# Four graph layers on one core: features kept times 2048, statistics behind the last additions, and pass one's first four tiles summed by portions

## The reference

```
x += segment_sum(w[e] * gate(h) * (h @ W0) [src], dst)                          # layer 0
x += segment_sum(h[src], dst) @ W1.T + b1                                       # layer 1
agg = segment_sum(concat(h[src], h[dst]) @ Wm + bm, dst)
x += concat(h, agg) @ Wu + bu                                                   # layer 2
e = B_inv * segment_sum((h @ W3)[src], dst);  y = D_inv * segment_sum(e[dst], src) + b3
x += relu(batchnorm(y))                                                         # layer 3
```

## Time and profile before

| | us |
|---|---|
| median of 3 runs | 2575.72 (2571.42 to 2576.82) |
| the profiled execution | 2590.25 |
| its span, first to last instruction | 2588.4 |
| TensorE busy | 2311.7 (89%) |
| VectorE busy | 1599.1 (62%) |
| ScalarE busy | 1218.6 (47%) |
| mean granted TensorE clock | 0.958 of full |

### The profile page before, as it was taken

How to read it: one execution, slowest core, us unless ns; L and a number is a source line. 1 busy time by engine, 2 the same in 40 slices (tenths; PEclk the granted TensorE clock), 3 DMA queues, 4 the chain that set the end, 5 groups by cost and what they waited for, 6 DMA issues and landing times. The chain is left out here.

```text
span 2588.4 us, 71075 instructions
## 1 busy us (share of the span) xinstructions
PE 2311.7 (89%) x27901; PEld 1993.6 (77%) x27901; DVE 1599.1 (62%) x3654; ACT 1218.6 (47%) x2644; POOL 45.6 (2%) x51
## 2 busy tenths in 40 slices
PE   2489899999989998999938999899998999999997
PEld 2368788878778887887837888788887888887786
DVE  6689999999999998999962333234433222122223
ACT  2478787877778886887732222222232000011112
POOL 3300000000000000000000000000000000000000
PEclk9589999999999999999979999999999999999998
DMA  6579999999999999999999999899997999999997
GB/s 190 110 152 204 208 208 207 215 217 210 201 193 216 213 213 201 196 215 209 207 229 232 283 284 281 227 260 259 260 258 203 290 288 290 274 246 245 256 267 186
DMA packets 1608975, 589.27 MB, mean 228 GB/s; under 512 B 964422, under 2 KB 1605450, under 8 KB 1608567
## 3 DMA queue, kind: packets, MB, share of 16 engines
q1 hardware_dynamic: 1604869, 579.88, 100.7%
q0 software_dynamic: 1600, 4.92, 0.7%
q10 hardware_dynamic: 2226, 0.62, 0.2%
HBM read 255.26 MB, written 89.20 MB: 133 GB/s over the span
## 5 line engine op out<-in xcount | busy, mean ns | idle before, releaser
L1182 ACT CAST stage<-ps 128x784 f16<-128x784 f32 x784 | 656.5, 837 | 108.5 <-DMA counts_by_source<-stage 69.5
L655 PE MATMUL ps<-Ha,a_tiles 128*128 128x258 f16 x4802 | 548.2, 274 | 46.4 <-ACT Ha L1229 38.9
L655 PEld LDWEIGHTS ps<-Ha,a_tiles 128*128 128x128 f16 x4802 | 469.9, 98 | 116.5 <-ACT Ha L1229 39.1
L608 PE MATMUL ps<-hot_c,hot_r 128*128 128x98 f16 x3136 | 509.8, 212 | 13.6 <-DVE hot_c L890 7.3
L609 PE MATMUL ps<-hot_c,hot_r 128*128 128x98 f16 x3136 | 504.1, 211 | 0.0
L610 PE MATMUL ps<-hot_c,hot_r 128*128 128x98 f16 x3136 | 502.3, 210 | 0.0
L1167 ACT CAST stage<-ps 128x392 f16<-128x392 f32 x784 | 398.8, 509 | 141.5 <-PE ps L591 141.5
L583 PE MATMUL ps<-g_in,wt 128*128 128x128 f16 x2401 | 431.4, 222 | 34.7 <-DVE X L902 18.2
L584 PE MATMUL ps<-g_in,wt 128*128 128x128 f16 x2401 | 429.4, 222 | 0.0
L585 PE MATMUL ps<-g_in,wt 128*128 128x128 f16 x2401 | 429.2, 222 | 0.0
L902 DVE SCALAR_TENSOR_TENSOR X<-ps,X 128x512 f32<-128x512 f32 (+1 forms) x637 | 391.6, 649 | 52.1 <-PE ps L585 51.9
(11 more groups left out here) (195 smaller groups left out, 2039.8 us busy)
## 6 DMA issues: line engine op xcount, KB each, us to landing
a_tiles<-counts_by_source SPq DMA_DIRECT2D x147, 1600.0 KB, 8.8
counts_by_source<-stage SPq DMA_DIRECT2D x49, 1600.0 KB, 8.0
gated_parts<-G SPq DMA_DIRECT2D x7, 448.0 KB, 3.6
g_in<-gated_parts SPq DMA_DIRECT2D x98, 32.0 KB, 3.1
out_x<-X SPq DMA_DIRECT2D x12, 256.0 KB
edge_table<-tab SPq DMA_DIRECT2D x1, 2448.0 KB, 10.5
wt<-stage SPq DMA_TRANSPOSE x98, 10.9
dst_run<-in_dst SPq DMA_DIRECT2D x1, 612.4 KB
```

The lines of the kernel that those rows point to most:

```text
L608: mm(into(0), rows_, codes(0), start=v == 0, stop=True, skip_group_check=True)
L655: last = mm(ps[:, c % 2, 0:PARTS], a_slot(ph, c, i), moving[:, i], start=i == 0, stop=i == TILES - 1)
L1182: a.copy(stage[:, b, 0:2, 0:TILES, u * SET_COLS:(u + 1) * SET_COLS], of).then_inc(s("hi_done"), 1)
```

## The change

- Features are kept times 2048. The standard deviation is taken of var / 2048^2 + eps / 2048^2, so `rstd`, `nmr` and all features come out times 2048. The high part is the value times 1/2048 in float16, and one VectorE instruction (scalar_tensor_tensor, high * -2048 + value) writes the low part straight to Ha or Hb. ScalarE's low parts (L1208, L1229, L1258), the buffer `dbig` and the waits between them go. To make up for it `w_h` is multiplied by 1/2048, in one instruction ahead of the build, and `binv` by 2048.
- Statistics stand between the additions of tile 48: those of group g - 1 behind the addition of group g.
- Pass one: sums of the first four tiles are made together, each in a bank of its own. TensorE waits for the loads of all four, then for one portion at a time, and does the seven matmuls of that portion for each of the four tiles. Their transposes and weights follow after that.

The places left out repeat the same with `sum_bank`, drop the allocation of `dbig` and rename semaphores.

```diff
@@ -40,6 +40,7 @@
 LOW = 2048.0
+TOGETHER = 4
 WIDE = P + 2
@@ -93,6 +94,11 @@
     return (ph - 1) * TILES + c
+
+
+def sum_bank(ph, j, c):
+
+    return j if ph == 1 and isinstance(j, int) and j < TOGETHER else c % 2
...
@@ -470,6 +475,7 @@
             g.memset(cols[:, 5:6], EPS).then_inc(s("eps"), 1)
+            g.memset(cols[:, 6:7], EPS / (LOW * LOW)).then_inc(s("eps"), 1)
             g.memset(pad_rows[0:1, 0, :], 0).then_inc(s("pads"), 1)
@@ -640,9 +646,24 @@
+                    def first_tiles():
+
+                        for j in range(TOGETHER):
+                            pe.wait_ge(s(f"a_in{load_at(1, j) % SLOTS}"), (load_at(1, j) // SLOTS + 1) * 16)
+                        for part in range(SET):
+                            pe.wait_ge(s("h_ready1"), part + 1)
+                            for j in range(TOGETHER):
+                                for i in range(part * SET, (part + 1) * SET):
+                                    last = mm(ps[:, sum_bank(1, j, j), 0:PARTS], a_slot(1, j, i), Ha[:, i], start=i == 0, stop=i == TILES - 1, skip_group_check=True)
+                                if part == SET - 1:
+                                    last.then_inc(s("sum_done1"), 1)
+
                     def step(j, k, c, ph=ph, moving=moving):
                         q = c % SLOTS
-                        if on(j) and not general:
+                        if ph == 1 and not general and isinstance(j, int) and j < TOGETHER:
+                            if j == 0:
+                                first_tiles()
+                        elif on(j) and not general:
                             if ph == 4:
...
@@ -682,7 +703,8 @@
                     else:
-                        pe.wait_ge(s(f"h_ready{ph}"), SET if ph == 1 else TILES)
+                        if ph > 1:
+                            pe.wait_ge(s(f"h_ready{ph}"), TILES)
                     if not (general and ph == 3):
...
@@ -911,6 +933,12 @@
+                def row_stats(g):
+
+                    dve.wait_ge(s("added"), FOURS * (TILES - 1) + g + 1)
+                    for i in range(4 * g, min(4 * g + 4, TILES)):
+                        v.bn_stats(stats[:, i], X[:, i])
+
                 if general:
@@ -919,8 +947,11 @@
                     dve.wait_ge(s("g_x"), 1)
+                    for j in range(TILES):
+                        v.bn_stats(stats[:, j], X[:, j])
                 else:
                     dve.wait_ge(s("g_parts"), SET)
+                    v.tensor_scalar(w_h[:], w_h[:], 1.0 / LOW, None, ALU.mult)
                     tiles_loop(dve, build, 0)
@@ -928,22 +959,18 @@
                             add_four(t, t % 2, g)
-                    dve.wait_ge(s("added"), FOURS * TILES)
-                for j in range(TILES):
-                    v.bn_stats(stats[:, j], X[:, j])
-
-                def split(ph):
-
-                    if ph == 1:
-                        counts_stored(dve)
+                            if t == TILES - 1 and g:
+                                row_stats(g - 1)
+                    row_stats(FOURS - 1)
+                def split():
+
+                    counts_stored(dve)
                     for c in range(SET):
-                        dve.wait_ge(s(f"split_h{ph}"), c + 1)
-                        to = Ha[:, c * SET:(c + 1) * SET, 0:P]
-                        v.tensor_copy(to, hbig[:, c % 2]).then_inc(s(f"split_hi{ph}"), 1)
-                        dve.wait_ge(s(f"split_hi{ph}"), c + 1)
-                        if c >= 2:
-                            dve.wait_ge(s(f"h_ready{ph}"), c - 1)
-                        v.tensor_tensor(dbig[:, c % 2], hbig[:, c % 2], to, ALU.subtract).then_inc(s(f"split_d{ph}"), 1)
+                        dve.wait_ge(s("split_h"), c + 1)
+                        tiles = slice(c * SET, (c + 1) * SET)
+                        v.tensor_scalar(Ha[:, tiles, 0:P], hbig[:, c % 2], 1.0 / LOW, None, ALU.mult).then_inc(s("split_hi"), 1)
+                        dve.wait_ge(s("split_hi"), c + 1)
+                        v.scalar_tensor_tensor(Ha[:, tiles, P:2 * P], Ha[:, tiles, 0:P], -LOW, hbig[:, c % 2], ALU.mult, ALU.add).then_inc(s("h_ready1"), 1)
@@ -954,7 +981,7 @@
                         dve.wait_ge(s("new_row"), t + 1 + (ph - 1) * TILES)
-                        v.tensor_scalar(part(to, t, 0, P), hnew[:, z, 0], 1.0, None, ALU.mult).then_inc(s("new_high"), 1)
+                        v.tensor_scalar(part(to, t, 0, P), hnew[:, z, 0], 1.0 / LOW, None, ALU.mult).then_inc(s("new_high"), 1)
                     if on(j, 2):
@@ -964,7 +991,7 @@
                         dve.wait_ge(s("new_high"), t + 1 + (ph - 1) * TILES)
-                        v.tensor_tensor(hnew[:, z, 1], hnew[:, z, 0], part(to, t, 0, P), ALU.subtract).then_inc(s("new_rest"), 1)
+                        v.scalar_tensor_tensor(part(to, t, P, 2 * P), part(to, t, 0, P), -LOW, hnew[:, z, 0], ALU.mult, ALU.add).then_inc(s(f"h_ready{ph + 1}"), 1)
                     if on(j, 2):
...
@@ -1038,10 +1065,9 @@
                                 hi = Hb[:, j, 0:P] if isinstance(j, int) else Hb[:, bass.ds(j, 1), 0:P].rearrange("p a f -> p (a f)")
-                                e(v.tensor_copy(hi, upd[:, q, 0]))
-                                if later(j, SLOTS):
-                                    dve.wait_ge(s("h_ready4"), j - (SLOTS - 1))
-                                v.tensor_tensor(upd[:, q, 1], upd[:, q, 0], hi, ALU.subtract).then_inc(s("e_rest"), 1)
+                                e(v.tensor_scalar(hi, upd[:, q, 0], 1.0 / LOW, None, ALU.mult))
+                                lo = Hb[:, j, P:2 * P] if isinstance(j, int) else Hb[:, bass.ds(j, 1), P:2 * P].rearrange("p a f -> p (a f)")
+                                v.scalar_tensor_tensor(lo, hi, -LOW, upd[:, q, 0], ALU.mult, ALU.add).then_inc(s("h_ready4"), 1)
                             else:
...
@@ -1118,9 +1144,9 @@
-            def std(ph):
+            def std(ph, scale=1.0):
                 act.wait_ge(s("var"), ph + 1)
-                a.activation(t49[:, 1], t49[:, 1], ACT.Sqrt).then_inc(s("std"), 1)
+                a.activation(t49[:, 1], t49[:, 1], ACT.Sqrt, scale=scale).then_inc(s("std"), 1)
                 act.wait_ge(s("normed"), ph + 1)
...
@@ -1191,25 +1217,17 @@
-                    if on(j, 5):
-                        act.wait_ge(s("new_rest"), j - 4 + (ph - 1) * TILES)
                     if on(j, 4):
                         act.wait_ge(s("row_norm"), j - 3 + (ph - 1) * TILES)
                     if on(j, 3):
                         z = (c - 3) % SLOTS
                         act.wait_ge(s("row_var"), j - 2 + (ph - 1) * TILES)
-                        a.activation(sds[:, z:z + 1], mvs[:, z, 1:2], ACT.Sqrt, bias=cols[:, 5:6]).then_inc(s("row_std"), 1)
+                        a.activation(sds[:, z:z + 1], mvs[:, z, 1:2], ACT.Sqrt, bias=cols[:, 6:7], scale=1.0 / (LOW * LOW)).then_inc(s("row_std"), 1)
                     if on(j, 4):
                         relu_row(hnew[:, (c - 4) % SLOTS, 0], j - 4).then_inc(s("new_row"), 1)
-                    if on(j, 5):
-                        t, z = j - 5, (c - 5) % SLOTS
-                        to = Hb if ph == 1 else Ha
-                        lo = to[:, t, P:2 * P] if isinstance(t, int) else to[:, bass.ds(t, 1), P:2 * P].rearrange("p a f -> p (a f)")
-                        a.activation(lo, hnew[:, z, 1], ACT.Copy, scale=LOW).then_inc(s(f"h_ready{ph + 1}"), 1)
-
                 for ph in (1, 2, 3, 4):
                     if ph == 1 or (general and ph < 4):
-                        std(ph)
+                        std(ph, 1.0 if general else 1.0 / (LOW * LOW))
                         if general:
@@ -1217,16 +1235,12 @@
                             counts_stored(act)
-                        for c in range(SET + 1):
-                            if c < SET:
-                                if c >= 2:
-                                    act.wait_ge(s(f"split_d{ph}"), c - 1)
-                                for i in range(SET):
-                                    last = relu_row(hbig[:, c % 2, i], c * SET + i)
-                                last.then_inc(s(f"split_h{ph}"), 1)
-                            if c:
-                                act.wait_ge(s(f"split_d{ph}"), c)
-                                a.activation(Ha[:, (c - 1) * SET:c * SET, P:2 * P], dbig[:, (c - 1) % 2], ACT.Copy, scale=LOW).then_inc(s(f"h_ready{ph}"), 1)
+                        for c in range(SET):
+                            if c >= 2:
+                                act.wait_ge(s("h_ready1"), c - 1)
+                            for i in range(SET):
+                                last = relu_row(hbig[:, c % 2, i], c * SET + i)
+                            last.then_inc(s("split_h"), 1)
...
@@ -1251,11 +1265,6 @@
                             next_rows(ph, j, c)
-                        if ph == 3 and on(j, 1):
-                            t, d = j - 1, c - 1
```

(24 more changed lines are left out.)

## The result

The changed kernel takes 2566.28 us in the median of 12 runs, the kernel before 2574.86; the ratio is 0.9959 (95% interval 0.9946 to 0.9972). In a second session it was 0.9953 (0.9935 to 0.9971). The forecast was 2569.0, from a gain of 6.7 us. One of the twelve runs of the kernel before took 4598.36 us; the ratio leaves it out, and without it that median is 2574.01.

The account below looks back on a forecast made before the run. TensorE, busy 89% of the span, and its standstills were taken as the bound. Terms: -6.7 + 0.7 - 0.35 - 0.35 - 0.2 + 0.2 = -6.7 us, from the median 2575.72 to 2569.0; range 2563 to 2576.5.

Parts of the forecast that it names:

- Statistics behind the additions: Tile 48 ahead of pass one: 1.38 us a group, statistics end 2.25 us sooner, last addition 6.4 us later.
- the second rival: VectorE doesn't overlap unlike instructions: 1.79 us a group, TensorE starts 2.3 us sooner, time 2573.4; chance 0.15.
- The loads set the start: Start of pass one: a_tiles' fourth load lands at 1359.1, TensorE starts about 1359.2, 6.7 us sooner; chance 0.63.
- the landing at 1352.7: Fourth load of a_tiles if loads weren't held back; the start of pass one could then be 13 us sooner.
- Direct low part: VectorE writes it, two 1.09 us instructions a portion; saves 0.35 us ahead of passes two and three, 0.2 at four.
- The chain behind four tiles and the clock: Pass one before tile 4: exposed transpose, copies and addition cost 0.7 us, bounds 0 and 1.5; low-clock price left unchanged.
- Slots: Loads of a_tiles in pass one: tile 0's slot comes free later, yet a margin of about 6 us holds.
- The slower rival: Pass one runs out of loads; at 6.2 us a load it costs 11 us, time 2580; chance 0.05.
- rival 3: Shifted code changes TensorE's issue stalls: one more costs 6 us, time 2575, chance 0.12; one fewer gives 2563, chance 0.03.
- the 0.2 ahead of M: Scaling w_h on VectorE just ahead of the build's first one-hot: 0.2 us later, bounds 0 and 0.44.

Follow-up runs that it names:

- second trace: The kernel before and the changed kernel, each unchanged and profiled once more; ratios to the kernel before 0.9992 and 0.9953.

## Why the prediction held, step by step

**Statistics behind the additions: right.** 1.37 us a group for 1.38, statistics done 2.4 us sooner against M for 2.25, last addition 6.3 us later for 6.4.

**The section on the pipeline of VectorE.** The Trainium skill, "VectorE: DVE Perf Modes", section "The DRAIN you can't avoid", says that the next operation does not start until the pipeline is empty. Taken alone, that gives the second rival, groups at 1.79 us and a start 2.3 us sooner. The prediction took it alone and passed over an exception: the same section adds that a next operation that is not held starts earlier. The trace agrees with the exception: unlike instructions started 0.60 us after the start of one that lasts 0.69. The second rival is out.

**The loads set the start: right, and shown.** 42.2 for 42.1 (1359.2 - 1317.08), released by a load; undoing the statistics moved it by 6.2 us, freeing the loads by 11.7. The last portion was ready at M + 41.2 for 41.5. What I did not draw from my own working was its price tag: I had the landing at 1352.7 without the statistics in hand and left it as a bound.

**Direct low part: right at the hand-overs.** Two instructions of 1.09 us a portion, as costed. The step from portion to portion is 2.69 for 2.71. TensorE's waits ahead of passes two, three and four shrank by 0.35, 0.57 and 0.21 us (7.20, 7.50 and 2.16 before; 6.85, 6.93 and 1.95 now), for 0.35, 0.35 and 0.2. But of what it gave ahead of pass three nothing reached the end: pass two with that wait took 0.5 us longer in the changed kernel (325.0 us from its first matmul to that of pass three, 324.5 before). Ahead of pass three TensorE's clock was already low: in the last 10 us of this stretch the granted clock was 0.50 on average for 0.67 before. Alone, the start came 4.3 us sooner, where my formula says 5.2; additions that ended 0.9 us later in that trace make up the difference.

**The chain behind four tiles and the clock: mis-sized.** I put 0.7 us and it was 1.5, the end of the bounds that I gave. The chain itself took 1.6 us for the 1.5 that I had reckoned. The rest is the clock: the prediction left its price as it was and allowed a microsecond either way. By windows (columns as in the earlier trace rows), the changed kernel:

```profile
1348.00:1350.00 2.00, 2.00 (x12) 1.39 (x10) 0.00 (x0) 0.00 (x0) 0.00 (x0) 0.50 1.16 290
1350.00:1352.00 2.00, 2.00 (x17) 1.64 (x16) 0.00 (x0) 0.00 (x0) 0.00 (x0) 0.85 1.16 291
```

and the kernel before:

```profile
1370.00:1372.00 2.00, 2.00 (x19) 1.73 (x18) 0.00 (x0) 0.00 (x0) 0.00 (x0) 0.98 0.00 0
```

and the changed kernel with the statistics after all additions, which started at 1334.30:

```profile
1336.00:1338.00 2.00, 2.00 (x12) 1.45 (x11) 1.51 (x2) 2.00 (x6) 0.00 (x0) 0.55 1.16 291
1338.00:1340.00 2.00, 2.00 (x21) 1.74 (x19) 1.49 (x3) 1.71 (x5) 0.00 (x0) 1.00 1.16 290
```

TensorE stayed at 1.2 GHz for about 5.7 us after its start instead of 4.2, after a standstill in both, and for 3.5 us in the third kernel. (These times are estimates, from the mean granted clock of windows of half a microsecond.) In the seven kernels with portions, tile 4 begins 25.1 to 26.3 us after the start. Where nothing interrupted the 196 matmuls they took 23.7 us after 3.5 us at the low clock (24.1 after 4.4, 24.2 after 4.6) and 24.9 after 6.0: half of each further microsecond at half the clock is lost, which is what the term lacked.

**Slots: right.** No wait for a_tiles shows after the first one. The slower rival, pass one out of loads, did not occur.

**A gain that my sum lacks.** A stall called issue, the kind that rival 3 counts on, took part, with the other sign and on another engine than I had it. VectorE's timeline behind the last pass, the kernel before (second trace):

```profile
2554.00 0.60 DVE L1099 BATCH_NORM_STATS2 stats<-OT 128x6 f32<-128x256 f32 x2 [2.55 <-issue]
2556.39 0.83 DVE L1102 BATCH_NORM_AGGREGATE fin<-stats 128x2 f32<-128x150 f32 x1 [1.79 <-issue]
```

and the changed kernel (second trace):

```profile
2549.50 0.60 DVE L1125 BATCH_NORM_STATS2 stats<-OT 128x6 f32<-128x256 f32 x2 [2.65 <-issue]
2550.13 0.83 DVE L1128 BATCH_NORM_AGGREGATE fin<-stats 128x2 f32<-128x150 f32 x1
```

The source of these lines is the same; the second stall, 1.8 us, is gone. It is there in all five traces of kernels without the direct low part (1.76 to 2.12 us) and in none of the eight with it. Where VectorE's code lies may be the reason, but that is not shown; no run moved the code alone. The first stall, 2.3 to 2.7 us, is in all thirteen.

The sum from M, in means of the two traces of each kernel: start -6.6, four tiles +1.6, from there to pass two's start -0.5, pass two +0.5, pass three with the start of pass four -0.2, pass four -0.3, and what stands behind its last tile, where the stall went, -1.6. That makes -7.1 (7.6 in the first pair of traces, 6.6 in the second; pass four alone differs by 1.4 us between the two traces of the kernel before). The forecast had -6.9 there (-6.7 with the 0.2 ahead of M). The start, by far the largest term, and its mechanism were right and are shown. That the total came out as close is partly luck: the four tiles cost 0.9 us more than forecast and pass two gave back 0.9 less, and a gain of 1.6 us that the forecast did not know made up for both.

## What to carry to other kernels

Before work is put between two instructions of an engine, look for who waits for the later one: here eleven groups of statistics filled VectorE's pauses and finished 2.4 us sooner, while the additions behind them, and with them every load of the next stage, came 6.3 us later. A wait on "all of that work" in front of a transfer is often wider than what the memory needs; split by what each buffer overlays, it gave 15 us here behind M, twice what the change gave, and 18 together with a wait by tile. And an edit's worth has a sign only beside its neighbours: the same interleaving moved the start of pass one 2.4 us forward alone, 6.2 back beside the portions, and 2.9 forward once the loads were free.

## What the runs showed of the hardware that I had not expected

- Stalls named issue come and go with no change to the code near them: 15.5 us in the setup stage of one execution and none in the next of the same kernel; 1.76 to 2.12 us behind the last pass, there in all five traces without the direct low part and in none of the eight with it. The traces name no cause.
- The low clock after a standstill of TensorE lasted between about 3.5 and 6.0 us in traces of nearly the same stretch (the 196 matmuls of the four tiles without a pause), enough to move one step by 1.2 us.
